# Turning the gated low-rank rows on DVE in 32x32 blocks instead of on PE

## The reference

```python
y      = einsum('bct,bcd->bdt', x, cond_weights[itok])    # a 64x64 mix of the channels, per batch
base   = y @ W_base.T + b_base                            # 1024 -> 1024
route  = weights of the top 2 of 8 experts, from softmax(y @ W_gate.T)
h      = einsum('bnd,erd->bner', y, A)                    # 8 experts x rank 16 = 128 columns
hw     = h * route[..., None]                             # the gated low-rank rows
out    = x + base + einsum('bner,eor->bno', hw, B)        # the low-rank part, scaling 1
```

## Time and profile before

| | us |
|---|---|
| median of 3 runs | 950.12 (949.57 to 950.32) |
| the profiled execution | 950.2 |
| its span | 948.4 |
| PE busy | 936.9 (99%) |
| POOL busy | 548.3 (58%) |
| DVE busy | 432.8 (46%) |
| ACT busy | 383.4 (40%) |
| one pass of the loop | 29.02 |

### The profile page before, as it was taken

How to read it: one execution, slowest core, us unless ns; L and a number is a source line. 1 busy time by engine, 2 the same in 40 slices (tenths; PEclk the granted TensorE clock), 3 DMA queues, 4 the chain that set the end, 5 groups by cost and what they waited for, 6 DMA issues and landing times.

```text
span 948.4 us, 16849 instructions
## 1 busy us (share of the span) xinstructions
PE 936.9 (99%) x5462; PEld 880.4 (93%) x5462; DVE 432.8 (46%) x1333; ACT 383.4 (40%) x815; POOL 548.3 (58%) x514
## 2 busy tenths in 40 slices
PE   8989999999999999999999999999999999999998
PEld 6979999999999999999999999999999999999997
DVE  5884444443444434444434444344443344443444
ACT  6734334433434333343334343433433343433332
POOL 2885556555466555565554765555655547555560
PEclk9999999999999999999999999999999999999999
DMA  9333322233322333222333223332223332233312
GB/s 309 125 112 122 133 101 90 88 119 133 114 98 87 110 122 133 97 92 88 122 133 111 99 88 111 122 133 92 94 90 122 133 111 99 89 111 122 133 48 86
DMA packets 41452, 107.13 MB, mean 113 GB/s; under 512 B 4449, under 2 KB 8674, under 8 KB 41442
## 3 DMA queue, kind: packets, MB, share of 16 engines
q1 hardware_dynamic: 41440, 107.01, 32.4%
q10 hardware_dynamic: 2, 0.00, 0.0%
HBM read 73.43 MB, written 33.55 MB: 113 GB/s over the span
## 4 chain that ended last, share of the span: by engine, by line
PE 92%; POOL 3%; issue 1%; DMA 1%; SPq 1%; DVE 1%; POOLq 0%; ACT 0%; DVEq 0%
PE ps L801 54%; PE ps_r L801 18%; PE ps_out L819 10%; PE ps_out L829 9%; DMA w_sum<-in_w_t 1%; POOL a_lo L308 1%; PE ps_hwt L825 1%; POOL s_lo L312 1%; POOL s_sum L333 0%; POOLq L342 0%; POOL mix L346 0%; SPq L220 0%; POOL s_sum L319 0%; POOL s_sum L325 0%; SPq L224 0%
## 5 line engine op out<-in xcount | busy, mean ns | idle before, releaser
L308 POOL TENSOR_TENSOR a_lo<-raw,a_hi 128x512 fp32r<-128x512 f32 x128 | 164.9, 1310 | 239.5 <-ACT a_hi L410 239.4
L620 DVE TENSOR_TENSOR z_sum<-ps,z_sum 128x448 f32<-128x448 f32 x155 | 96.9, 625 | 242.0 <-PE ps L801 241.9
L801 PE MATMUL ps<-w_hi,s_hi 128*128 128x448 f32 x496 | 183.7, 370 | 1.5 <-DVE z_sum L620 1.1
L801 PE MATMUL ps<-w_lo,s_hi 128*128 128x448 f32 x496 | 181.2, 365 | 0.0
L801 PE MATMUL ps<-w_hi,s_lo 128*128 128x448 f32 x496 | 179.7, 362 | 0.0
L801 PE MATMUL ps_r<-r_lo,a_hi 128*128 128x264 f32 x496 | 140.9, 284 | 0.0
L801 PE MATMUL ps_r<-r_hi,a_hi 128*128 128x264 f32 x496 | 140.7, 284 | 0.0
L801 PE MATMUL ps_r<-r_hi,a_lo 128*128 128x264 f32 x496 | 140.6, 283 | 0.0
L801 PE MATMUL ps<-w_hi,a_hi 128*128 128x448 f32 x372 | 138.5, 372 | 0.0
L801 PE MATMUL ps<-w_lo,a_hi 128*128 128x448 f32 x372 | 135.2, 363 | 0.0
L801 PE MATMUL ps<-w_hi,a_lo 128*128 128x448 f32 x372 | 135.0, 363 | 0.0
(11 more groups left out here) (97 smaller groups left out, 1596.4 us busy)
## 6 DMA issues: line engine op xcount, KB each, us to landing
raw<-in_x_t SPq DMA_DIRECT2D x128, 256.0 KB, 2.7
o_sb<-in_x SPq DMA_DIRECT2D x64, 512.0 KB, 3.6
out_x<-o_sb SPq DMA_DIRECT2D x62, 512.0 KB, 2.7
w_sum<-in_w_t SPq DMA_DIRECT2D x8, 448.0 KB, 9.7
r_raw<-in_w_t SPq DMA_DIRECT2D x4, 264.0 KB, 4.4
table_raw<-in_cond_w SPq DMA_DIRECT2D x2, 256.0 KB, 9.3
b_raw<-in_b_t SPq DMA_DIRECT2D x1, 512.0 KB, 10.6
out_x<-o_sb SPq DMA_DIRECT2D x2, 224.0 KB, 2.1
```

Source lines behind the costliest of these rows:

```text
L308: pool.tensor_tensor(a_lo[j][:], raw[j][:], as_f32(a_hi[j][:]), ALU.subtract).then_inc(s_a_lo[j], 1)
L620: return dve.tensor_tensor(to, bank[:, 0:NS], other, ALU.add)
L801: mm = pe.matmul(bank[:, 0:w.shape[-1]], a[:, k, :], w[:, k, :], start=(opens and k == 0 and q == 0), stop=(closes and k == KH - 1 and q = ...
```

## The change

For tiles 3 to 62 hw is transposed by DVE instead of PE. DVE's transpose works on 32x32 blocks, so a tile takes sixteen instructions, each writing block (c, r) of hwt_sum from block (r, c) of hw. hwt_sum is a tile in SBUF in the same place as hwt_lo; the subtraction is done in place. ACT casts hwt_hi from hwt_sum once all sixteen blocks are in. Tiles 0, 1, 2 and 63 keep the old way.

The sixteen of an odd tile stand at the end of the pass on DVE. Those of an even tile are cut in three: four after `weigh_experts`, four after the P5 sum, eight after z_lo of tile 1 Q.

```diff
-        hwt_lo = sb("hwt_lo", [P, P], F32R)
+        hwt_sum, hwt_lo = shared("hwt_sum", "hwt_lo", [P, P])
...
             def hwt_top(i):
-                act.wait_ge(s_hwt, i + 1)
+                act.wait_ge(s_turned, BLOCKS * (i - 2))
+                act.copy(hwt_hi[:], hwt_sum[:]).then_inc(s_hwt_hi, 1)
+
+            def pe_hwt_top(n):
+                act.wait_ge(s_hwt, n)
                 act.copy(hwt_hi[:], ps_hwt[:, 0:P]).then_inc(s_hwt_hi, 1)
...
-            def hwt_rest(i):
+            def turn_hw(i, parts=range(P // TURN)):
+                dve.wait_ge(s_hw, i + 1)
+                for c in parts:
+                    for r in range(P // TURN):
+                        dve.transpose(hwt_sum[c * TURN:(c + 1) * TURN, r * TURN:(r + 1) * TURN],
+                                      hw[r * TURN:(r + 1) * TURN, c * TURN:(c + 1) * TURN]).then_inc(s_turned, 1)
+
+            def hwt_rest(i, whole=hwt_sum[:]):
                 dve.wait_ge(s_hwt_hi, i + 1)
-                dve.tensor_tensor(hwt_lo[:], ps_hwt[:, 0:P], as_f32(hwt_hi[:]), ALU.subtract).then_inc(s_hwt_lo, 1)
+                dve.tensor_tensor(hwt_lo[:], whole, as_f32(hwt_hi[:]), ALU.subtract).then_inc(s_hwt_lo, 1)
...
                 add(ps_6, p1, u3).then_inc(s_u3, 1)
                 weigh_experts(p, 0)
+                turn_hw(2 * p, (0,))
                 dve.wait_ge(s_p[5], p + 1)
                 dve.wait_ge(s_u3, p)
                 add(ps_5, u3, u3).then_inc(s_z_sum[1, Q], 1)
+                turn_hw(2 * p, (1,))
                 added_rest(p, 1, Q)
+                turn_hw(2 * p, (2, 3))
                 dve.wait_ge(s_p[4], p + 1)
...
                 weigh_experts(p, 1)
+                turn_hw(2 * p + 1)
...
                 strassen(ps_6, s2_hi, s2_lo, T2, True).then_inc(s_p[6], 1)
-                turn_hw(2 * p - 1)
                 pe.wait_ge(s_p1_out, p)
...
-                strassen(ps_5, s2_hi, s2_lo, B22, False, lambda: turn_hw(2 * p)).then_inc(s_p[3], 1)
+                strassen(ps_5, s2_hi, s2_lo, B22, False).then_inc(s_p[3], 1)
```

More of the change, by code:

```diff
@@ L23 @@
 A11, A12, A21, A22 = range(4)
+TURN = 32
+BLOCKS = (P // TURN) ** 2
 WARM_UP = 10
@@ L184, in adaln_ffn @@
         s_hw = sem("hw_ready")
-        s_hwt = sem("hwt_ready")
+        s_hwt = sem("hwt_in_psum")
+        s_turned = sem("hwt_blocks_turned")
         s_hwt_hi = sem("hwt_hi_ready")
@@ L487, in _ @@
             sum_top(1, 1, s1[:], s1_hi)
-            hwt_top(0)
+            pe_hwt_top(1)
             act.wait_ge(s_p[3], 1)
@@ L506, in first @@
                 t_top(2, T2)
-                hwt_top(1)
+                pe_hwt_top(2)
                 t_top(3, T3)
@@ L525, in first @@
                 added_top(1, 1, L)
-                hwt_top(2)
+                pe_hwt_top(3)
                 added_top(1, 0, Q)
@@ L578, in _ @@
             pairs(act, first, step)
-            hwt_top(TILES - 1)
+            pe_hwt_top(4)
             act.wait_ge(s_r_sum[1], PAIRS)
@@ L695, in _ @@
             dve.tensor_tensor(b_lo[:], b_raw[:], as_f32(b_hi[:]), ALU.subtract).then_inc(s_b_lo, 1)
-            hwt_rest(0)
+            hwt_rest(0, ps_hwt[:, 0:P])
             z_rest(0, 0, Q, ps_5[:, 0:NS])
@@ L712, in first @@
             def first():
-                hwt_rest(1)
+                hwt_rest(1, ps_hwt[:, 0:P])
                 z_rest(1, 0, L, ps_1[:, 0:NS])
@@ L738, in first @@
                 added_rest(1, 1, L)
-                hwt_rest(2)
+                hwt_rest(2, ps_hwt[:, 0:P])
                 dve.wait_ge(s_p[3], 2)
@@ L749, in first @@
                 weigh_experts(1, 1)
+                turn_hw(3)
             def step(p, last):
@@ L786, in step @@
                 weigh_experts(p, 1)
+                turn_hw(2 * p + 1)
             pairs(dve, first, step)
-            hwt_rest(TILES - 1)
+            hwt_rest(TILES - 1, ps_hwt[:, 0:P])
             z_rest(PAIRS - 1, 1, R, ps_r[:, 0:width[R]])
```

## The result

| | before | after |
|---|---|---|
| median, us | 950.22 (4 runs) | 1084.26 (4 runs) |
| ratio, 95% interval | | 1.1419 (1.1405 to 1.1432) |
| profiled execution, its span | 950.2, 948.4 | 1083.57, 1081.6 |

The direction was forecast (slower, at a chance of 0.70), the size was not: 970.6 us was given, with 984 as the upper end, and the loss is 133 us of span in place of 20.

A forecast was written before the change was run, and what follows sets the result against it. PE, busy 99% of the span, was taken as the bound. Each pass 0.90 + 0.02 - 0.24 = +0.68 us, over 30 passes +20.4 us on 950.2, gave 970.6 us, range 943 to 984.

The forecast's parts named there:

- What is removed: PE's queue: 60 transposes gone at 0.12 us each, -7.2 us in all, -0.24 us a pass.
- What is added, d: DVE's sixteen 32x32 turns a tile: time from one start to the next, taken as 0.20 us, bounds 0.08 and 0.28.
- L: Lateness of the even tile's P4 sum on DVE behind the turns, passed on to hwt_lo: 0.90 us a pass.
- the two reasons given: Why DVE turns run end to end: no streaming into the successor, and another partition block read each turn; 0.20 us apart.
- I take 0: ACT's read and DVE's subtraction from SBUF instead of a bank: 0.01 to 0.05 us more, priced at 0.
- the price of z_lo: DVE's z_lo behind the even tile's second four turns: starts 0.16 us late, still 0.67 us long.
- The third rival: DVE turns of 0.25 us or more, from two phases or POOL in the way: 990 to 1003 us; chance 0.07.
- The price of a late hwt_lo: PE's low-rank matmuls waiting for the even tile's hwt_lo: PE loses L + 0.02 us a pass.
- The stall forecast: PE waiting on hwt_lo in each of 30 passes, somewhat longer than today's 0.5 us (matmuls) and 0.9 us (weight loads).
- The odd tile's price of 0: Odd tile's sixteen turns, 3.2 us, fit into DVE's 4.38 us wait for P6 and cost nothing.
- three signs of being wrong: Turns under 0.135 us apart, DVE's lateness not reaching hwt_lo, or the odd tile's sixteen outlasting 4.38 us.

The follow-up runs named there:

- odd_only: Changed kernel with only odd tiles 3 to 61 turned by DVE, even tiles given back to PE; 946.86 us, ratio 0.9968 to the kernel before.
- early_lo2: Changed kernel with twelve turns together behind the P5 sum and the even tile's hwt_lo moved ahead of both z_lo; 943.73 us, ratio 0.9937.
- pool_after: Changed kernel with only POOL reordered: S3's s_lo behind the S2 sum, which waits for the even tile's hwt_lo; 984.26 us, ratio 1.0362.
- rows_outer: Changed kernel with the two loops over the blocks exchanged, so in odd tiles the written block changes each turn; 1084.27 us.
- same_block2: Changed kernel with all sixteen turns reading and writing the first 32 partitions, low-rank result not right; 945.42 us.
- psum_turn: Changed kernel with the turns written into the bank ps_hwt instead of SBUF, ACT and DVE reading the bank; 1031.41 us, ratio 1.0854.
- block_copies2: Changed kernel with each turn replaced by a plain copy of the block, low-rank result not right; 1149.93 us.
- idle_4: Kernel before, with PE's transposes, plus four 1024-column DVE memsets in front of each pass's P4 sum; 1102.94 us.

## Why the prediction was wrong

- **What is removed** was right to within 1 us: 0.12 us a transpose, 7.2 us in all. odd_only gained 3.1 for half of them and early_lo2 6.3 for all.
- **What is added, d.** Right in kind (end to end) and somewhat small: 0.234 in place of 0.20. With POOL out of the way this makes L = 1.34 in place of 0.90 and 34 us in place of 20.4: 13 us of the error. Of the two reasons given, the first, that a transpose cannot stream into its successor, was wrong: within one block it does, at 0.09 us. The second, that each turn reads another partition block than the one before, was right.
- **"I take 0" for the change of hwt_lo from a bank to a second SBUF tile** is the step that failed, together with the price of z_lo. I had compared durations of the two forms in rows where POOL happened not to be first. hwt_lo's second SBUF input cost 1.06 us a pass, z_lo, moved by 0.34 us, 0.91, and 0.17 is left, of which 0.12 lies at the z_lo behind it: 2.14 x 30 = 64 us. pool_after took away just this much, 32.28 - 30.15 = 2.13 us a pass. The third rival came nearest: it had POOL get in the way, but of the turns, which POOL did not lengthen, and it was dismissed because "POOL works beside DVE already". The step also passed over a row of the kernel before, POOL's s_lo of 1.69 us in place of its usual 1.29.
- **The price of a late hwt_lo** was right to 0.01 us a pass (L + 0.02, from one row in pair 1).
- **The clock** was not thought of: the sum has no term for it. 23 passes of 1.54 us, 35 us. The stall forecast, L = 0.90 less the 0.25 us by which the stall is shorter than L (1.09 for 1.34, 3.22 for 3.48), is by this estimate 0.65 us, and no stall of up to 1.1 us made it fall.
- The sum: 34 from the turns (20 forecast), 64 from the ports, 35 from the clock, 133 us.
- **The odd tile's price of 0** was right: 3.71 of the 4.38 us, with PE not waiting.
- None of the prediction's three signs of being wrong came (turns under 0.135 us apart, a lateness that does not reach hwt_lo, an odd tile that outlasts the 4.38 us): the error lay in instructions beside the turns, at which none of them looked.

## What to carry to other kernels

When an edit moves an elementwise instruction on DVE by a few tenths of a microsecond, or gives it a second SBUF input, look at what POOL runs at that moment: of the two, the one that started later was the one held up here, and a small shift can turn round which of them that is. Many small instructions that change their partition block do not overlap; count them at their full duration and put them where the engine waits anyway, and take whatever does not depend on the moved chain out from behind it. A stall of PE that comes in every pass can have a second price, the lower clock after it (here with stalls of 2.0 us and more, not with 1.1), so the loss does not grow in proportion to the stall.

## What the runs showed of the hardware

- A 32x32 fp32 transpose on DVE: 0.203 us long from SBUF to SBUF and 0.234 from start to start when the partition block changes on either side (the changed kernel, rows_outer), 0.09 from start to start when it does not (same_block2); into a bank 0.223 and 0.256 (psum_turn).
- A plain copy of 32x32 that changes its block: 0.20 from start to start, and four of them took 3.94 us while POOL worked (block_copies2).
- DVE with two SBUF inputs against POOL: 0.62 to 0.67 us becomes 1.50 to 1.58 (448 columns), 0.28 becomes 1.34 (128 columns). POOL's 1.29 becomes 1.69 where DVE's z_lo started first. With one input in a bank hwt_lo stayed at 0.28 beside a running POOL instruction, and the turns themselves, with a single SBUF input, were not lengthened.
- PE's clock fell to its lower level after none of the stalls of 0.9 to 1.1 us, after a sixth to a third of those of 2.0 to 2.2, after 23 of 28 of 3.2 and after all of 3.5 us. It cost 1.54 us a time for the stalls of 2.0 to 3.2 us, an estimated 1.4 in idle_4. Why one stall of 3.2 us is followed by it and the next is not stays open.
